# Finding the capacity threshold of eight experts: ten rounds of four or six candidates in place of eight rounds of seven

## The chip, the cores and the metric

The kernel runs on one core of a Trainium2 chip. The metric is the device time of one execution in microseconds, median of several runs. One execution was recorded by the hardware profiler; "span" is the time from its first to its last recorded instruction. The engines are TensorE (PE for its matmuls, PEld for its weight loads), VectorE (DVE), ScalarE (ACT), GpSimd (POOL) and SyncE (SP), which here only issues transfers.

## The reference, cut to what matters

64 sequences of 128 tokens with 128 features go through a layer norm, a cross-attention block with ternary weights and 8-bit activations and a residual addition. Then comes a second layer norm and a mixture of eight experts, which the change belongs to:

```python
T = tokens.shape[0]                                 # 8192
capacity = int(math.ceil(T / E * 1.25))             # 1280, E = 8
logits = tokens @ router_w.T
probs = jax.nn.softmax(logits, axis=-1)
top1_idx, top1_prob = argmax(probs), max(probs)
order = jnp.lexsort((-top1_prob, top1_idx))         # by expert, the most probable first
...
keep = (position in the expert's group) < capacity
final_e = where(keep, top1_idx, 0)                  # the rest fall back to expert 0
for e in range(E):
    h = relu(tokens @ W1[e] + b1[e]); y = h @ W2[e] + b2[e]
    out = out + where(final_e == e, y, 0)
```

A token keeps its expert if it is among the 1280 most probable tokens of that expert.

## The kernel before, in words

The program is one straight line per engine, put in order by hand. Semaphores order the engines among each other. The stages are: loading and quantising (to about 90 us), attention (to about 190 us), the quantised feed-forward block with residual, second layer norm and logits (to about 294 us), routing (to about 374 us), and the expert passes to the end.

**Routing.** After the softmax every token has a key, minus its top probability times `FULL` = 2^26, in the column of its own expert and 0 elsewhere (L1540). The sorting of the reference is replaced by a search: for each expert the kernel looks for the key value at which the count of tokens at or below it reaches the capacity. The keys are turned by TensorE (L1078) so that the 128 partitions hold eight experts times sixteen parts, 512 keys in each, once in PSUM bank 0 (read by VectorE) and once in bank 3 (read by ScalarE).

The search has `LEVELS` = 8 rounds, `level(k)` on VectorE from L1549. A round narrows the interval of each expert to one eighth: 

- There are `WAYS - 1` = 7 candidates, in the columns of `cand`. VectorE counts for four of them (`VECTOR_COUNTS`, L1546, 128x512, with the sum in `cnt`), ScalarE for three (L798, Sign of candidate minus key, with the sum in `cnt`).
- When both are done, TensorE adds the sixteen parts of each expert (L1087, `same_expert` times `cnt`) onto a row of offsets, `enough`, that an earlier matmul (L1083) has put into the same bank: minus the capacity for VectorE's counts, `T - 2 * CAP` for ScalarE's, whose sum of signs runs from -8192 to 8192. A candidate has reached the capacity where the result is at least 0.
- VectorE counts these (L1559, `reached` and `met`), makes the next candidates (L1562, from `met`, `minus_w` and `base`, which L1557 prepared while TensorE was at work), and moves the threshold `thr` (L1564).
- Both engines wait for `cand` (semaphore `s_cand`), and TensorE waits for both (`s_cnt`, `s_cnt_act`, in `count_up`).

The width of the steps is 2^26 divided by 8, by 64 and so on, to 4 in the eighth round. After it VectorE alone counts for the four single units below (L1571 to L1578), and the threshold is exact to one unit.

The constants `nth` (1, 2, 3, ...), `minus_w` and `enough` are written by GpSimd at the start of the program (L524 to L528).

**After the search** VectorE works out ties, each token's place in its expert's list and the index tables (L1596 to L1675), with a few matmuls of TensorE between. It ends with `src_of` and `slot_of`, behind which the semaphore `s_idx` lets GpSimd start.

**The expert passes.** GpSimd's queue gathers 64 tiles of 128 token rows by an indirect transfer (L587) and scatters 64 tiles of results (L594), from the 32nd gather on in turns. SyncE copies the weights of the pass's expert (L490). TensorE, ScalarE and VectorE compute 71 passes (L1131, L1138, L1147 with L816, L828, L1697, L1703, L1709).

Of the kernel before, what the change touches and what calls it, by code (L numbers as in the profile page):

```python
# [11 lines left out]
ALU = mybir.AluOpType  # L12
# [3 lines left out]
P = 128  # L16
# [9 lines left out]
T = B * S  # L26
# [6 lines left out]
CAP = int(np.ceil(T / NX * 1.25))  # L33
# [20 lines left out]
MAGIC = 12582912.0  # L54
EPS = 1e-5
FULL = 2.0 ** 26
WAYS = 8
LEVELS = 8
VECTOR_COUNTS = 4
EXP_IS_ONE = -2.0 ** -25  # L60
HT = 16
FAR = 32768
# [49 lines left out]
def xattn_moe(nc, x, ctx_in, weights, biases, router_w, W1, b1, W2, b2, out):  # L112
    rows = nc.dram_tensor("token_rows", (T, XW), F32).ap()
    with ExitStack() as stack:
        def sb(name, shape, dtype=F32):
            return stack.enter_context(nc.sbuf_tensor(name, shape, dtype))

        def sem(name):
            return stack.enter_context(nc.semaphore(name))
# [6 lines left out]
        ones = sb("ones", [P, P])  # L126
# [6 lines left out]

        nth = sb("nth", [P, WAYS - 1])
        minus_w = sb("minus_w", [P, LEVELS])
        enough = sb("enough", [1, WAYS - 1])
        tile_no_b = sb("tile_no_b", [P, TILES], BF16)
        row_no_b = sb("row_no_b", [P, P], BF16)
        part_no = sb("part_no", [P, 1])
# [77 lines left out]
        def route(n):  # L217
            return big[:, n * 512:(n + 1) * 512]
# [30 lines left out]
        by_pass = big[:, 10 * 512:10 * 512 + 4 * PASSES].rearrange("p (k a) -> p k a", a=PASSES)  # L249
        cnt = sb("cnt", [P, WAYS - 1])  # L250
        reached = sb("reached", [P, WAYS - 1])
        thr_row = sb("thr_row", [NX, NX])
        above_row = sb("above_row", [P, NX])
        met = sb("met", [P, 1])
        base = sb("base", [P, WAYS - 1])
        thr = sb("thr", [P, 1])
        cand = sb("cand", [P, WAYS - 1])
        thr8 = sb("thr8", [P, NX])
# [14 lines left out]
        s_const = sem("constants_made")  # L273
# [86 lines left out]
        s_cand = sem("candidates_ready")  # L360
# [31 lines left out]
        def bank(n, width=512, rows_=P):  # L392
            return psum[0:rows_, n, 0:width]
# [101 lines left out]
        def _(pool):  # L495
# [20 lines left out]
            for d in range(-(P // NX) + 1, P // NX):  # L516

                pool.affine_select(out=same_expert[:, :], in_=same_expert[:, :], compare_op=ALU.not_equal, fill=1.0,
                                   base=NX * d, pattern=[[-1, P]], channel_multiplier=1).then_inc(s_cc, 1)
                pool.wait_ge(s_cc, 5 + d + P // NX)  # L520
            segv = seg[:, :].rearrange("p (e t) -> p e t", e=NX)
            pool.memset(segv[:, :, 0:1], 0.0).then_inc(s_const, 1)
            for k in range(LEVELS):
                pool.memset(minus_w[:, k:k + 1], -FULL / WAYS ** (k + 1)).then_inc(s_const, 1)  # L524
            pool.memset(enough[:, 0:4], float(-CAP)).then_inc(s_const, 1)
            pool.memset(enough[:, 4:WAYS - 1], float(T - 2 * CAP)).then_inc(s_const, 1)
            pool.iota(nth[:, :], pattern=[[1, WAYS - 1]], base=1, channel_multiplier=0,
                      allow_small_or_imprecise_dtypes=True).then_inc(s_const, 1)  # L528
            for e in range(NX):
# [77 lines left out]
        def _(act):  # L607
# [17 lines left out]
            w = CJ * DC // NP  # L625
# [61 lines left out]
            w = T // XP  # L687
# [105 lines left out]
            act.wait_ge(s_vt, 2)  # L793
            for k in range(LEVELS):
                if k:
                    act.wait_ge(s_cand, k)
                for j in range(VECTOR_COUNTS, WAYS - 1):
                    m = act.activation(route(5 + j), bank(3), ACT.Sign, bias=cand[:, j:j + 1], scale=-1.0,  # L798
                                       accum_out=cnt[:, j:j + 1])
                m.then_inc(s_cnt_act, 1)  # L800
# [42 lines left out]
        def _(pe):  # L843
# [71 lines left out]
            w = T // XP  # L915
# [164 lines left out]

            def count_up(k, n):

                pe.matmul(bank(1 + k % 2, n), ones[0:1, :], enough[:, 0:n], start=True, stop=False)  # L1083
                pe.wait_ge(s_cnt, k + 1)
                if k < LEVELS:
                    pe.wait_ge(s_cnt_act, k + 1)
                pe.matmul(bank(1 + k % 2, n), same_expert[:, :], cnt[:, 0:n], start=False, stop=True  # L1087
                          ).then_inc(s_cnt2, 1)

            for k in range(LEVELS):  # L1090
                count_up(k, WAYS - 1)
            count_up(LEVELS, 4)
            pe.wait_ge(s_thr, 1)
            pe.matmul(bank(4, NX), ones[0:NX, :], thr_row[:, :], start=True, stop=True).then_inc(s_thr_s, 1)
# [69 lines left out]
        def _(dve):  # L1164
            ch = Chain(dve, s_dve)

            def do(ins):
                ch.link(ins)
                ch.join()
# [45 lines left out]
            w = CJ * DC // NP  # L1215
# [134 lines left out]
            w = T // XP  # L1350
# [180 lines left out]
            do(dve.tensor_reduce(t64[2][:, :], v3(route(1)), AX, ALU.max))  # L1531
            ch.link(dve.tensor_tensor(v3(route(1)), v3(route(1)), over_e(t64[2][:, :]), ALU.is_equal))
            ch.link(dve.memset(thr[:, :], 0.0))
            ch.link(dve.tensor_scalar(cand[:, :], nth[:, :], -FULL / WAYS, None, ALU.mult))
            dve.wait_ge(s_ex, 1)
            ch.link(dve.tensor_copy(w1b[:, :, FF:FF + NC], b1col))
            do(dve.tensor_reduce(t64[1][:, :], v3(route(4)), AX, ALU.add))
# [7 lines left out]
            def count(column, limit, form):  # L1545
                return dve.tensor_scalar(route(5 + column).bitcast(I16)[:, 0:512], key, limit, None, form, ALU.add,  # L1546
                                         accum_out=cnt[:, column:column + 1])

            def level(k):  # L1549

                w = FULL / WAYS ** (k + 1)
                for j in range(VECTOR_COUNTS):
                    m = count(j, cand[:, j:j + 1], ALU.is_le)
                m.then_inc(s_cnt, 1)
                if k + 1 < LEVELS:
                    ch.join()
                    do(dve.tensor_scalar(base[:, :], nth[:, :], -w / WAYS, thr[:, :], ALU.mult, ALU.add))  # L1557
                dve.wait_ge(s_cnt2, k + 1)
                do(dve.tensor_scalar(reached[:, :], bank(1 + k % 2, WAYS - 1), 0.0, None, ALU.is_ge, ALU.add,  # L1559
                                     accum_out=met[:, :]))  # L1560
                if k + 1 < LEVELS:
                    dve.scalar_tensor_tensor(cand[:, :], minus_w[:, k:k + 1].to_broadcast([P, WAYS - 1]), met[:, :],  # L1562
                                             base[:, :], ALU.mult, ALU.add).then_inc(s_cand, 1)
                    ch.link(dve.scalar_tensor_tensor(thr[:, :], met[:, :], -w, thr[:, :], ALU.mult, ALU.add))  # L1564
                    dve.wait_ge(s_cand, k + 1)
                else:
                    do(dve.scalar_tensor_tensor(thr[:, :], met[:, :], -w, thr[:, :], ALU.mult, ALU.add))

            for k in range(LEVELS):
                level(k)  # L1570
# [63 lines left out]
            first, start, end = spans[:, 0, :], spans[:, 1, :], spans[:, 2, :]  # L1634
# [28 lines left out]
            w = [big[:, (14 + j) * 512:(14 + j) * 512 + TILES] for j in range(2)]  # L1663
# [84 lines left out]
```

## Time and profile before

| | us |
|---|---|
| median of 3 runs | 544.47 |
| lowest and highest | 543.80, 544.93 |
| the profiled execution | 545.08 |
| its span | 543.3 |

| engine | busy us | share of the span | instructions |
|---|---|---|---|
| PE | 378.2 | 70% | 2861 |
| DVE | 377.3 | 69% | 941 |
| ACT | 353.1 | 65% | 827 |
| POOL | 197.7 | 36% | 276 |

No engine is busy all the time: these shares are averages over stages with different limits. The chain of waits, followed back from the last instruction, tells what set the end in each stage, and the timeline of a stretch shows the instructions with the idle time before each and what ended it. The profiled execution's 545.08 us stand 1.8 us above its span and 0.6 us above the median.

### The profile page before, as it was taken

The page shows a single profiled execution, that of the slowest core. Times are in us where ns is not written, and L with a number is a line of the kernel's source. Part 1 is how long each engine was busy: PE and PEld are TensorE (multiplying, and loading weights), DVE is VectorE, ACT ScalarE, POOL GpSimd, SP SyncE. Part 2 cuts the span into 40 slices and gives each one's busy share as a digit, 9 for nine tenths or more (in the row PEclk, how much of TensorE's full clock was granted, in tenths as well). Part 3 has the DMA queues.
Part 4 walks back from the last instruction along what each step waited for, and adds up shares of the span by engine and source line. Part 5 has one row for each costly group of instructions (what it writes and reads, how often), then busy time and mean ns, then how long its engine had stood idle before and what let it go on. Part 6 is the DMA issues. An engine that isn't in the chain of part 4 may idle for free.

```text
span 543.3 us, 10418 instructions
## 1 busy us (share of the span) xinstructions
PE 378.2 (70%) x2861; PEld 307.1 (57%) x2861; DVE 377.3 (69%) x941; ACT 353.1 (65%) x827; POOL 197.7 (36%) x276
## 2 busy tenths in 40 slices
PE   0370418999999889957876322233999999998940
PEld 0230005689999744426553222032999999998940
DVE  2999998478888869967898788796355555444520
ACT  1589987687878549949983443052677777776720
POOL 7300093244444300000000000003777777777774
PEclk9999999999999969978989555568799999999985
DMA  9920000000000000000336950002767666665511
GB/s 216 246 71 1 1 0 0 2 1 2 0 0 0 1 1 1 0 0 1 80 79 121 256 129 0 1 1 83 226 224 230 224 226 223 216 233 198 201 54 34
DMA packets 45137, 48.67 MB, mean 90 GB/s; under 512 B 10232, under 2 KB 32800, under 8 KB 45088
## 3 DMA queue, kind: packets, MB, share of 16 engines
q1 hardware_dynamic: 39728, 38.59, 24.0%
q0 software_dynamic: 4096, 8.46, 5.9%
q10 hardware_dynamic: 1264, 1.03, 0.7%
q8 instruction: 23, 0.38, 0.3%
q14 instruction: 26, 0.21, 0.1%
HBM read 16.20 MB, written 8.45 MB: 45 GB/s over the span
## 4 chain that ended last, share of the span: by engine, by line
PE 48%; DVE 23%; ACT 15%; DMA 5%; issue 4%; POOL 3%; SPq 0%; DVEq 0%; POOLq 0%; ACTq 0%
PE psum L1138 11%; PE psum L1147 10%; PE psum L956 6%; PE psum L972 5%; DVE big L1546 4%; PE psum L964 2%; ACT xqT L759 2%; POOL out L594 2%; DMA keys<-in_ctx 2%; ACT tok_b L759 2%; ACT big L662 2%; DMA out<-xall,src_of 2%; DVE xqT L1628 2%; DVE part L1322 2%; ACT big L619 1%
## 5 line engine op out<-in xcount | busy, mean ns | idle before, releaser
L587 POOL DMA_INDIRECT xall<-token_rows,src_of x64 | 61.7, 964 | 202.7 <-DVE slot_of L1675 183.5
L828 ACT ACTIVATE xqT<-psum,feat 128x128 f32<-128x128 f32 x284 | 81.0, 368 | 32.6 <-PE psum L1138 30.7
L1138 PE MATMUL psum<-xqT,feat 128*128 128x128 f32 x568 | 77.3, 281 | 0.0
L1147 PE MATMUL psum<-keys,xqT 128*128 x568 | 75.7, 277 | 0.3 <-issue 0.2
L1138 PEld LDWEIGHTS psum<-xqT,feat 128*128 128x128 f32 x568 | 71.4, 198 | 0.0
L594 POOL DMA_INDIRECT out<-xall,src_of x64 | 62.9, 983 | 19.5 <-issue 11.0
L1147 PEld LDWEIGHTS psum<-keys,xqT 128*128 128x128 f32 x568 | 68.9, 192 | 1.3 <-issue 0.9
L1703 DVE TENSOR_TENSOR xqT<-psum,feat 128x128 f32<-128x128 f32 x71 | 20.7, 292 | 52.2 <-PE psum L1147 51.7
L561 POOL TENSOR_TENSOR qb<-qb,arec 128x308 f32<-128x308 f32 x32 | 21.8, 699 | 64.6 <-DVE arec L1380 64.6
L972 PE MATMUL psum<-probT,keys 78*128 78x128 f32 x256 | 35.3, 285 | 1.8 <-ACT probT L724 1.8
L1697 DVE TENSOR_SCALAR xqT<-xall 128x128 f32 x71 | 25.8, 363 | 12.1 <-DMA xall<-token_rows,src_of 11.1
L972 PEld LDWEIGHTS psum<-probT,keys 78*128 78x128 f32 x256 | 32.1, 196 | 3.5 <-ACT probT L724 2.7
L1709 DVE SCALAR_TENSOR_TENSOR xall<-xqT,in_pass,xall 128x128 f32 x71 | 25.1, 353 | 11.8 <-ACT xall L822 9.1
L956 PE MATMUL psum<-keys 128*128 128x77 f32 x256 | 32.1, 277 | 1.3 <-ACT keys L609 0.9
L956 PEld LDWEIGHTS psum<-keys 128*128 128x128 f32 x256 | 30.0, 192 | 4.2 <-ACT keys L609 1.6
L724 ACT COPY probT<-psum 77x512 f32<-77x512 f32 x32 | 18.3, 576 | 21.0 <-PE psum L964 21.0
L850 PE MATMUL psum<-ident,amax 128*1 128x128 f32 x6 | 2.2, 372 | 40.6 <-DVE amax L1222 15.4
L609 ACT ACTIVATE keys<-psum,bcol,scale 128x308 f32<-128x308 f32 (+1 forms) x48 | 28.3, 658 | 3.1 <-PE psum L932 3.0
L816 ACT COPY xqT<-psum 128x128 f32<-128x128 f32 x71 | 20.5, 289 | 13.0 <-PE psum L1131 12.8
L798 ACT ACTIVATE big<-psum,cand 128x512 f32<-128x512 f32 x24 | 16.2, 683 | 18.5 <-DVE cand L1562 12.8
L1131 PE MATMUL psum<-ident,xqT 128*128 128x128 f32 x71 | 20.3, 286 | 7.9 <-DVE xqT L1697 7.9
L1546 DVE TENSOR_SCALAR_CACHE_REDUCE big<-psum,cand 128x512 int16<-128x512 f32 x36 | 24.9, 748 | 1.2 <-PE psum L1078 1.2
(301 smaller groups left out, 933.9 us busy)
## 6 DMA issues: line engine op xcount, KB each, us to landing
feat<-keys SPq DMA_DIRECT2D x71, 322.0 KB
token_rows<-xall SPq DMA_DIRECT2D x4, 1040.0 KB, 8.1
xall<-in_x SPq DMA_DIRECT2D x8, 512.0 KB, 7.3
keys<-in_L_ffn_W SPq DMA_DIRECT2D x1, 2048.0 KB, 13.2
keys<-in_L_ffn_W SPq DMA_DIRECT2D x8, 256.0 KB, 7.5
keys<-in_ctx SPq DMA_DIRECT2D x4, 462.0 KB, 6.8
xall<-token_rows,src_of POOLq DMA_INDIRECT x64
out<-xall,src_of POOLq DMA_INDIRECT x64, 2.3
```

Source lines behind the costliest of these rows:

```text
L561: pool.tensor_tensor(pr, pr, arec[:, l, :].unsqueeze(2).to_broadcast([P, GB, CT]), ALU.mult).then_inc(s_p[l], 1)
L587: pool.indirect_dma_start(xring[:, t % RING, :], None, rows, bass.IndirectOffsetOnAxis(ap=src_of[:, t:t + 1], axis=0)).then_inc(s_g[t % TU ...
L594: pool.indirect_dma_start(out_rows, bass.IndirectOffsetOnAxis(ap=src_of[:, t:t + 1], axis=0), yring[:, t % RING, :], None).then_inc(s_o[t ...
L609: return act.activation(dst, src_bank, ACT.Identity, bias=bcol[:, b:b + 1], scale=scale[:, k:k + 1])
L828: m = act.activation(hT[a % DEPTH][:, P * c:P * c + P], bank(2 + a % 2)[:, P * c:P * c + P], ACT.Relu, bias=w_now[a % AHEAD][:, FF + c:FF ...
L956: m = pe.matmul(bank(1 + l)[:, CT * b:CT * b + CT], src[n % GR][:, P * b:P * b + P], kT[l][n % GR][:, CT * b:CT * b + CT], start=True, sto ...
L972: m = pe.matmul(bank(5 + l)[:, P * b:P * b + P], ktok[l][n % (GR if l else 2)][:, P * b:P * b + P], probT[l][:, P * b:P * b + P], start=Tr ...
L1138: m = pe.matmul(bank(2 + a % 2)[:, P * c:P * c + P], w_now[a % AHEAD][:, P * c:P * c + P], gT[a % DEPTH], start=True, stop=True)
L1147: m = pe.matmul(bank(4 + a % 2, E), hT[a % DEPTH][:, P * c:P * c + P], w2s[:, bass.ds(e, 1), c, :].rearrange("p e d -> p (e d)"), start=(c ...
L1546: return dve.tensor_scalar(route(5 + column).bitcast(I16)[:, 0:512], key, limit, None, form, ALU.add, accum_out=cnt[:, column:column + 1])
L1697: dve.tensor_scalar(gn[m], xr[:, 0:E], xr[:, E:E + 1], xr[:, E + 1:E + 2], ALU.subtract, ALU.mult).then_inc(s_prep, 1)
L1709: dve.scalar_tensor_tensor(y, yt[a % 2], in_pass[:, a:a + 1], y, ALU.mult, ALU.add).then_inc(s_y, 1)
```

## The change

The rounds become ten, with a radix of their own each: two rounds that divide by seven (six candidates) and eight that divide by five (four candidates). VectorE counts for the first half of a round's candidates and ScalarE for the other half. The steps are 4 times the product of the radices still to come, so 10,937,500 in the first round, 1,562,500 in the second, then 312,500 and so on down to 20 and 4. All of them are whole units. The four single units at the end stay. The row of offsets gets three forms: for four candidates, for six, and for the four of the end, where all counts are VectorE's.

```diff
-WAYS = 8
-LEVELS = 8
-VECTOR_COUNTS = 4
+RADIX = (7, 7) + (5,) * 8
+LEVELS = len(RADIX)
+STEP = [4.0 * int(np.prod(RADIX[k + 1:])) for k in range(LEVELS)]
+WAYS = max(RADIX)
+FORMS = sorted(set(RADIX)) + [LEVELS]
...
-        enough = sb("enough", [1, WAYS - 1])
+        enough = sb("enough", [1, len(FORMS), WAYS - 1])
...
             for k in range(LEVELS):
-                pool.memset(minus_w[:, k:k + 1], -FULL / WAYS ** (k + 1)).then_inc(s_const, 1)
-            pool.memset(enough[:, 0:4], float(-CAP)).then_inc(s_const, 1)
-            pool.memset(enough[:, 4:WAYS - 1], float(T - 2 * CAP)).then_inc(s_const, 1)
+                pool.memset(minus_w[:, k:k + 1], -STEP[k]).then_inc(s_const, 1)
+            for n, radix in enumerate(FORMS[:-1]):
+                half = radix // 2
+                pool.memset(enough[:, n, 0:half], float(-CAP)).then_inc(s_const, 1)
+                pool.memset(enough[:, n, half:2 * half], float(T - 2 * CAP)).then_inc(s_const, 1)
+            pool.memset(enough[:, len(FORMS) - 1, 0:4], float(-CAP)).then_inc(s_const, 1)
...
             for k in range(LEVELS):
                 if k:
                     act.wait_ge(s_cand, k)
-                for j in range(VECTOR_COUNTS, WAYS - 1):
+                for j in range(RADIX[k] // 2, RADIX[k] - 1):
                     m = act.activation(route(5 + j), bank(3), ACT.Sign, bias=cand[:, j:j + 1], scale=-1.0,
                                        accum_out=cnt[:, j:j + 1])
...
-                pe.matmul(bank(1 + k % 2, n), ones[0:1, :], enough[:, 0:n], start=True, stop=False)
+                form = FORMS.index(RADIX[k] if k < LEVELS else LEVELS)
+                pe.matmul(bank(1 + k % 2, n), ones[0:1, :], enough[:, form, 0:n], start=True, stop=False)
...
             for k in range(LEVELS):
-                count_up(k, WAYS - 1)
+                count_up(k, RADIX[k] - 1)
...
-            ch.link(dve.tensor_scalar(cand[:, :], nth[:, :], -FULL / WAYS, None, ALU.mult))
+            ch.link(dve.tensor_scalar(cand[:, :], nth[:, :], -STEP[0], None, ALU.mult))
...
-                w = FULL / WAYS ** (k + 1)
-                for j in range(VECTOR_COUNTS):
+                w, n = STEP[k], RADIX[k] - 1
+                for j in range(n // 2):
                     m = count(j, cand[:, j:j + 1], ALU.is_le)
                 m.then_inc(s_cnt, 1)
                 if k + 1 < LEVELS:
+                    more = RADIX[k + 1] - 1
                     ch.join()
-                    do(dve.tensor_scalar(base[:, :], nth[:, :], -w / WAYS, thr[:, :], ALU.mult, ALU.add))
+                    do(dve.tensor_scalar(base[:, 0:more], nth[:, 0:more], -STEP[k + 1], thr[:, :], ALU.mult, ALU.add))
                 dve.wait_ge(s_cnt2, k + 1)
-                do(dve.tensor_scalar(reached[:, :], bank(1 + k % 2, WAYS - 1), 0.0, None, ALU.is_ge, ALU.add,
+                do(dve.tensor_scalar(reached[:, 0:n], bank(1 + k % 2, n), 0.0, None, ALU.is_ge, ALU.add,
                                      accum_out=met[:, :]))
                 if k + 1 < LEVELS:
-                    dve.scalar_tensor_tensor(cand[:, :], minus_w[:, k:k + 1].to_broadcast([P, WAYS - 1]), met[:, :],
-                                             base[:, :], ALU.mult, ALU.add).then_inc(s_cand, 1)
+                    dve.scalar_tensor_tensor(cand[:, 0:more], minus_w[:, k:k + 1].to_broadcast([P, more]), met[:, :],
+                                             base[:, 0:more], ALU.mult, ALU.add).then_inc(s_cand, 1)
```

## Rows read from the trace of the kernel before

**Rows 1.** The page: the chain that ended last, its shares by line.

```profile
PE psum L1138 11%; PE psum L1147 10%; PE psum L956 6%; PE psum L972 5%; DVE big L1546 4%; PE psum L964 2%; ACT xqT L759 2%; POOL out L594 2%; DMA keys<-in_ctx 2%; ACT tok_b L759 2%; ACT big L662 2%; DMA out<-xall,src_of 2%; DVE xqT L1628 2%; DVE part L1322 2%; ACT big L619 1%
```

**Rows 2.** GpSimd, 374 to 544 us, by line: busy us, mean ns | idle us, what ended it.

```profile
L594 POOL DMA_INDIRECT out<-xall,src_of x64 | 62.9, 983 | 19.5 <-issue 11.0 <-DMA out<-xall,src_of 4.9 <-DVE xall L1709 3.7
```

**Rows 3.** Timeline, last stage: start us, duration us, instruction [idle before it <- releaser].

```profile
374.38 1.14 POOL L587 DMA_INDIRECT xall<-token_rows,src_of  x1 [183.47 <-DVE slot_of L1675]
...
536.72 0.97 POOL L594 DMA_INDIRECT out<-xall,src_of  x1 [0.30 <-DMA out<-xall,src_of]
```

**Rows 4.** Chain of waits through one round: start us, duration us, what.

```profile
310.73 2.75 DVE big L1546 x8
313.48 0.04 issue
313.52 0.61 PE psum L1087 x2
...
314.24 0.18 DVE reached L1559 x2
```

**Rows 5.** Timeline of the first round.

```profile
302.31 0.75 DVE L1546 TENSOR_SCALAR_CACHE_REDUCE big<-psum,cand 128x512 int16<-128x512 f32 x1 [1.21 <-PE psum L1078]
...
303.16 0.69 ACT L798 ACTIVATE big<-psum,cand 128x512 f32<-128x512 f32 x1 [5.64 <-PE psum L1078]
...
305.00 0.08 DVE L1546 DVE_READ_ACCUMULATOR big<-psum,cand 128x1 f32 x1
...
305.07 0.21 ACT L798 ACTIVATION_READ_ACCUMULATOR big<-psum,cand 128x1 f32 x1
...
305.42 0.57 PE L1087 MATMUL psum<-cnt,same_expert 128*128 128x7 f32 x2 [1.78 <-ACT big L798]
...
306.68 0.74 DVE L1546 TENSOR_SCALAR_CACHE_REDUCE big<-psum,cand 128x512 int16<-128x512 f32 x1
```

**Rows 6.** Timeline of the second and third rounds.

```profile
308.49 0.21 ACT L798 ACTIVATION_READ_ACCUMULATOR big<-psum,cand 128x1 f32 x1
308.69 0.09 DVE L1546 DVE_READ_ACCUMULATOR big<-psum,cand 128x1 f32 x1
...
309.50 0.60 PE L1087 MATMUL psum<-cnt,same_expert 128*128 128x7 f32 x2 [2.99 <-DVE big L1546]
...
310.69 0.75 DVE L1546 TENSOR_SCALAR_CACHE_REDUCE big<-psum,cand 128x512 int16<-128x512 f32 x1
...
311.94 0.20 ACT L798 ACTIVATION_READ_ACCUMULATOR big<-psum,cand 128x1 f32 x1
...
312.04 0.09 DVE L1546 DVE_READ_ACCUMULATOR big<-psum,cand 128x1 f32 x1
...
314.71 0.75 DVE L1546 TENSOR_SCALAR_CACHE_REDUCE big<-psum,cand 128x512 int16<-128x512 f32 x1
```

**Rows 7.** Timeline: the eighth round's first count, and the first of the single units.

```profile
330.79 0.75 DVE L1546 TENSOR_SCALAR_CACHE_REDUCE big<-psum,cand 128x512 int16<-128x512 f32 x1
...
334.92 0.75 DVE L1546 TENSOR_SCALAR_CACHE_REDUCE big<-psum,cand 128x512 int16<-128x512 f32 x1
```

**Rows 8.** The groups of 302 to 339 us: VectorE's small instructions of a round.

```profile
L1562 DVE SCALAR_TENSOR_TENSOR cand<-minus_w,met,base 128x7 f32<-128x7 f32 x7 | 1.6, 226 | 0.2
L1559 DVE TENSOR_SCALAR_CACHE_REDUCE reached<-psum 128x7 f32<-128x7 f32 x8 | 1.3, 166 | 5.4 <-PE psum L1087 5.4
```

**Rows 9.** Chain of waits ahead of the routing: ScalarE to TensorE.

```profile
293.38 0.59 ACT big L788
293.98 0.04 issue
```

**Rows 10.** Timeline of GpSimd after its constants.

```profile
66.65 1.76 POOL L550 TENSOR_TENSOR qb<-feat 128x704 f32<-128x704 f32 x1 [46.99 <-ACT feat L609]
```

**Rows 11.** Busy us by engine (instructions), then TensorE's granted clock, DMA share, GB/s.

```profile
301.00:303.00 2.00, 1.84 (x8) 1.56 (x8) 0.79 (x4) 0.00 (x0) 0.00 (x0) 0.50 1.05 379
...
318.70:322.80 4.10, 1.12 (x4) 1.00 (x4) 3.43 (x15) 2.16 (x7) 0.00 (x0) 0.50 0.01 3
```

**Rows 12.** Timeline: the same fp32 matmul of 128 columns at two granted clocks.

```profile
381.18 0.47 PE L1131 MATMUL psum<-ident,xqT 128*128 128x128 f32 x1 [1.17 <-DVE xqT L1697]
...
387.61 0.27 PE L1131 MATMUL psum<-ident,xqT 128*128 128x128 f32 x1
```

## The prediction, made before the changed kernel was run

> **What bounds the kernel now.** I read the page first. The engines' shares say little, since no engine passes 70%. The chain of waits says more: the counting of the search, L1546, is 4% of the chain that ended last [rows 1], so the search lies on the path that sets the end. Then I asked whether time won there reaches the end, so I read the last stage backwards. GpSimd's queue starts its first gather at 374.38, released by `slot_of`, and its last scatter ends at 536.72 + 0.97 = 537.69 [rows 3]. That is 163.31 us for 64 gathers and 64 scatters, 1.28 us each. The 64 scatters have 19.5 us of idle time before them, 0.30 each, which is what a mere issue costs, whatever the releaser's name [rows 2]. So this queue is full from its start to its end. Nothing else sets the length of the stage, and the whole stage moves with `slot_of`.
>
> Between the search and `slot_of` the chain is VectorE's, instruction behind instruction, with a few short matmuls. The transfers of expert weights that run beside the search are over by its fifth round: 3 GB/s from 318.7 on [rows 11]. So what the search gains, `slot_of` gains, and with it the end.
>
> **A round as it is.** The third round's first count starts at 310.69, the fourth's at 314.71: 4.02 us [rows 6]. Rows 4 show who sets it: four counts of VectorE and TensorE's sum. ScalarE's three counts end earlier and its name is not in the chain. I cut the round at TensorE's start, 313.52:
> - Counting: 313.52 - 310.69 = 2.83 us [rows 4, 6]. The pitch of VectorE's counts is 0.67, and TensorE starts 0.14 after the start of the last accumulator read.
> - The fixed part: from 313.52 to the next count at 314.71, 1.19 us. That is the two passes of the matmul (0.72 to `reached` at 314.24), then `reached`, `cand` and the hand-over (0.47) [rows 4, 6].
>
> The eighth round is 4.13 long, 330.79 to 334.92, since its candidates for the single units are made one after another [rows 7]. The first takes 306.68 - 302.31 = 4.37 [rows 5].
>
> **What the change makes of it, round by round.**
>
> First round, three and three. ScalarE starts late, at 303.16, because it waits for the second set of transposes, and its three counts end at 305.07 + 0.21 = 305.28. TensorE starts at 305.42, with ScalarE as the releaser; VectorE's fourth count was over at 305.08 [rows 5]. One count less on VectorE wins nothing. Gain 0.
>
> Second round, three and three. VectorE's third read starts at 308.69, which puts TensorE at 308.83. ScalarE's third read ends at 308.49 + 0.21 = 308.70, and with the 0.14 from its end to TensorE seen in the first round that is 308.84 [rows 5, 6]. Before it was 309.50. Gain 0.66.
>
> Rounds of two and two. Counted from 310.69, VectorE's second read starts at 312.04 (+1.35), so TensorE could start at +1.49. ScalarE's second read ends at 311.94 + 0.20 (+1.45), so TensorE could start at +1.59 with the same 0.14 [rows 5, 6]. The later one counts, 1.59 in place of 2.83: gain 1.24, and such a round is 1.59 + 1.19 = 2.78 us.
>
> The third to the eighth round of before become such rounds: 6 x 1.24 = 7.44. Two more rounds are added at 2.78: 5.56. The long hand-over to the single units now stands behind the tenth round and costs what it did. In sum 0 + 0.66 + 7.44 - 5.56 = 2.54 us less: 32.61 us of search (302.31 to 334.92) become 30.07.
>
> The uncertain term is the 0.14 from ScalarE's last accumulator read to TensorE, seen once. Another hand-over of this pair, L788 to a matmul, took 0.04 [rows 9]. At 0.04 VectorE would set the rounds of two and two at +1.49, 0.10 less each. With eight of them the gain would be 3.34. The other end is the 0.35 between the start of that read and TensorE [rows 5], in case the signal follows the read's end less closely than it did there: 0.21 more in eight rounds, 1.68, which leaves 0.86. I take 0.14, since it is this very instruction's.
>
> The instructions with six and four columns in place of seven I cost as before: `cand` takes 0.226 and `reached` 0.166 at seven columns [rows 8], and at most three columns of some 1 ns go. `base` stays hidden: in a short round it starts with the second read at +1.35 and TensorE's answer comes at +2.3. The row of offsets is put in place right behind the sum before, over a microsecond ahead of need. GpSimd's five more writes of constants lie ahead of an idle time of 46.99 us [rows 10]. The counts cost the same whatever the values of the candidates.
>
> A rule speaks against more and shorter rounds. The three small VectorE instructions of a round take 0.17 to 0.23 us each for at most seven columns [rows 8], so nearly all of it is a fixed price, and two rounds more pay it twice. The Trainium skill says why (VectorE: DVE Perf Modes, "The TRN2 errata"): each instruction pays a fixed latency between instructions, and many small tiles pay it per tile. The trace agrees in kind, but not in size: from the Trainium skill's table, 58 or 120 cycles and the columns, I estimate 0.07 us for `cand` and 0.13 for `reached`, so 0.20 where the rows have 0.47 with the hand-over. By the Trainium skill's figures the two added rounds would cost 0.54 less and the gain would be 3.1 us.
>
> **The time.** The profiled execution of 545.08 becomes 542.54. It lies 0.61 above the median of 544.47; with the same 2.54 the median becomes 541.93, 0.47% less. The measurement of this kernel can tell about 0.2%, 1.1 us, from no change.
>
> **The rivals.**
> - *ScalarE's hand-over is short.* VectorE sets the rounds, the gain is 3.34 and the time 541.1. For it: the 0.04 of rows 9. Against it: no accumulator is read there. Chance 0.16.
> - *The fixed part grows, and the change is slower.* In a round of two and two both engines end within 0.1 us, TensorE waits for both, and both wait for the same `cand`. The 1.33 us in which nobody counts (1.19 and 0.14) come ten times in place of eight. If ScalarE is released or read out later than in the rows, so that a short round takes over 2.78 + 2.54 / 8 = 3.10 us, the gain is gone. At 3.3 us per round the time would be 544.47 - 2.54 + 8 x 0.52 = 546.1. Against it: the third to seventh rounds of before agree to 0.01 us, and the slowest hand-over seen gives 2.99. Chance 0.05.
> - *The gain is given back behind the search.* If some transfer, and not `slot_of`, decided when GpSimd's queue moves, or its scatters came to wait for results, up to 2.5 us would be lost and the time would be 544.5. For it: 16 of the 64 scatters name an earlier scatter's landing as their releaser [rows 2]. Against it: each such wait is 0.30, as an issue with no wait. Chance 0.09.
> - *TensorE's clock comes back in the search.* It is at 0.50, 1.2 GHz, in the search, though TensorE was busy for 1.84 of 2 us just before it [rows 11]. A busy share of 1.12 in 4 becomes 1.12 in 2.8. At 2.4 GHz the fp32 matmul of 128 columns takes 0.27 in place of 0.47 [rows 12], so up to 0.2 a round, 2 us in all, and a time of 539.9. The Trainium skill (TensorE: Matmul & The Clock Gate, Part 1) has the clock throttled by default and released by activity; the rows of 301 to 303 show more activity than the new rounds will have, without a release. Chance 0.02.
>
> The forecast, a gain of 2.0 to 3.0, has 0.68.
>
> **How the numbers follow.** Faster by over 0.2% needs a time under 543.4: the forecast, the first and the last rival and a small part of the others, 0.87. Within 0.2%: 0.09. Slower: 0.04. The range of 8 in 10 reaches from the short hand-over with the median's own scatter of 0.5 below it, 540.6, to the long hand-over, 544.47 - 0.86 = 543.6.
>
> **What would show it.** In the profile after: ten rounds; the first 4.37 from first count to first count, the second 3.35, the others 2.78, the tenth 2.89; TensorE's L1087 released by ScalarE's L798 in all of them, where VectorE's L1546 released it eight times in nine before; 30.1 us from the first count to the first of the single units; the first gather 2.5 us earlier after the start of the search than now; the stage of GpSimd's queue unchanged at 163 us. The prediction is wrong in its main term if a short round takes over 3.1 us, and wrong in its path if the search is 2.5 us shorter and the time is not.

## The result and the profile after

The changed kernel takes 541.99 us in the median of 9 runs (541.48 to 542.93), the kernel before beside it 544.77 (9 runs, 543.45 to 546.08). The ratio is 0.9954, with an interval of 0.9942 to 0.9966: 1.9 to 3.2 us less. Forecast were 541.9 us. In a second comparison, on another occasion, the ratio was 0.9947 (0.9929 to 0.9964).

Here is the new search in the chain of waits of the changed kernel, one short round (start us, duration us, what). It answers to [rows 4].

```profile
311.97 1.46 ACT big L803 x4
313.42 0.14 issue
313.56 0.57 PE psum L1093 x2
314.13 0.03 issue
...
314.25 0.18 DVE reached L1566 x2
314.43 0.02 issue
314.45 0.23 DVE cand L1569
...
314.71 1.46 ACT big L803 x4
```

The counting in the chain is now ScalarE's (L803, L798 before), 1.46 us, where it was VectorE's, 2.75. After it comes an `issue` gap, time in which the engine waited for nothing that the profile shows, of 0.14 and no longer one of 0.04. From 311.97 to 314.71 a round takes 2.74 us. The waits of the changed kernel in the stretch from 298 to 340 us say the same of all ten rounds; the eleventh entry is the four single units (waiting engine <- engine waited for: us, times, longest).

```profile
PE psum L1093 <- ACT big L803: 17.5, 10, 2.3
...
PE psum L1093 <- DVE big L1552: 3.0, 1, 3.0
```

The timeline of the first round and the start of the second, third and fourth of the changed kernel answers to [rows 5, 6]:

```profile
301.54 0.75 DVE L1552 TENSOR_SCALAR_CACHE_REDUCE big<-psum,cand 128x512 int16<-128x512 f32 x1 [1.21 <-PE psum L1083]
...
302.39 0.69 ACT L803 ACTIVATE big<-psum,cand 128x512 f32<-128x512 f32 x1 [5.64 <-PE psum L1083]
...
304.30 0.21 ACT L803 ACTIVATION_READ_ACCUMULATOR big<-psum,cand 128x1 f32 x1
304.62 0.50 PEld L1093 LDWEIGHTS psum<-cnt,same_expert 128*128 128x128 f32 x2 [1.84 <-DVE big L1552]
304.65 0.57 PE L1093 MATMUL psum<-cnt,same_expert 128*128 128x6 f32 x2 [1.78 <-ACT big L803]
...
305.81 0.75 DVE L1552 TENSOR_SCALAR_CACHE_REDUCE big<-psum,cand 128x512 int16<-128x512 f32 x1
...
309.23 0.75 DVE L1552 TENSOR_SCALAR_CACHE_REDUCE big<-psum,cand 128x512 int16<-128x512 f32 x1
```

The first round is 4.27 us, the second 3.42, then come seven of 2.74 and the last of 2.85. Note that two engines are named at 304.62 and 304.65: the weight load gives VectorE as its releaser, the matmul ScalarE. ScalarE is the one that decides: VectorE's last read had ended at 303.64, ScalarE's ends at 304.51, and the weight load starts 0.11 behind that.

The stage behind is what it was. The first line answers to [rows 2] and the others, from the timeline of GpSimd, to [rows 3]:

```profile
L599 POOL DMA_INDIRECT out<-xall,src_of x64 | 63.0, 985 | 19.5 <-issue 11.3 <-DMA out<-xall,src_of 4.6 <-DVE xall L1716 3.7
```

```profile
370.72 1.13 POOL L592 DMA_INDIRECT xall<-token_rows,src_of  x1 [179.23 <-DVE slot_of L1682]
...
533.04 0.97 POOL L599 DMA_INDIRECT out<-xall,src_of  x1 [0.31 <-DMA out<-xall,src_of]
```

The granted clock stayed at 0.50, 1.2 GHz, through the short rounds (columns as in [rows 11]):

```profile
320.20:325.70 5.50, 2.14 (x8) 1.99 (x8) 4.02 (x20) 2.92 (x9) 0.00 (x0) 0.50 0.00 0
```

The spans of the two profiled executions differ by 543.3 - 539.6 = 3.7 us, more than the medians. Cut at the same places:

| stretch, us | before | after | gain |
|---|---|---|---|
| to the first count | 302.31 | 301.54 | 0.77 |
| search, to the first count of the single units | 32.61 | 29.72 | 2.89 |
| from there to GpSimd's first gather | 39.46 | 39.46 | 0.00 |
| GpSimd's queue, first to last | 163.31 | 163.29 | 0.02 |
| behind it | 5.61 | 5.59 | 0.02 |

The 0.77 lies ahead of everything that was changed, and in another execution of the same changed kernel this part ends at 302.57. It is no gain. The change's own gain in the trace is 2.89 us.

### The profile page after: what moved, and what is told of

Same layout as the page of the kernel before. It is cut to its first block, busy times and chain, and to the rows that moved or that the text cites. A ratio compares the mean times of both kernels' runs of the same rounds, so it can differ in the third digit from the quotient of the medians.

```text
span 539.6 us, 10429 instructions
## 1 busy us (share of the span) xinstructions
PE 377.7 (70%) x2869; PEld 306.5 (57%) x2869; DVE 372.4 (69%) x931; ACT 352.6 (65%) x823; POOL 197.4 (37%) x281
## 4 chain that ended last, share of the span: by engine, by line
PE 48%; DVE 22%; ACT 17%; DMA 5%; issue 4%; POOL 3%; SPq 1%; DVEq 0%; POOLq 0%; ACTq 0%
PE psum L1144 11%; PE psum L1153 11%; PE psum L961 6%; PE psum L977 5%; ACT big L803 3%; PE psum L969 2%; POOL out L599 2%; ACT tok_b L764 2%; DMA keys<-in_ctx 2%; ACT xqT L764 2%; ACT big L667 2%; DMA out<-xall,src_of 2%; DVE xqT L1635 2%; DVE part L1328 2%; ACT big L624 2%
## 5 line engine op out<-in xcount | busy, mean ns | idle before, releaser
L977 PEld LDWEIGHTS psum<-probT,keys 78*128 78x128 f32 x256 | 31.7, 193 | 3.5 <-ACT probT L729 2.7
L803 ACT ACTIVATE big<-psum,cand 128x512 f32<-128x512 f32 x22 | 14.9, 683 | 17.3 <-DVE cand L1569 11.7
L1028 PE MATMUL psum<-tok_b,f1T 128*128 128x512 bf16 x64 | 24.3, 380 | 2.2 <-ACT keys L757 1.3
```

Of the source, the lines that this page charges most:

```text
L977: m = pe.matmul(bank(5 + l)[:, P * b:P * b + P], ktok[l][n % (GR if l else 2)][:, P * b:P * b + P], probT[l][:, P * b:P * b + P], start=Tr ...
L1028: pe.matmul(bank(b), f1T[:, 0, P * c:P * c + P], tok_b[:, g4(i)], start=True, stop=False)
```

## The experiments

All are edits of the changed kernel. The table holds what the timelines and the comparisons gave; "search" runs from the first count to the first of the single units, the rounds in it are measured from first count to first count on VectorE. The ratio is to the kernel before, run on the same chip as the row's kernel, with its interval. The rows come from several chips, on which the kernel before had medians of 544.38 to 544.95.

| kernel | rounds, us | search | first gather to last scatter | median | ratio |
|---|---|---|---|---|---|
| before | 4.37, 4.01, 5 x 4.02, 4.13 | 32.61 | 163.31 | 544.77 | |
| changed | 4.27, 3.42, 7 x 2.74, 2.85 | 29.72 | 163.29 | 541.99 | 0.9954 (0.9942 to 0.9966) |
| changed, again | 4.27, 3.41, 7 x 2.74, 2.86 | 29.72 | 163.17 | 542.26 | 0.9947 (0.9929 to 0.9964) |
| share undone | 4.11, 4.01, 7 x 3.33, 3.45 | 34.90 | 163.25 | 547.27 | 1.0043 (1.0029 to 1.0058) |
| nine of seven | 4.27, 7 x 3.42, 3.53 | 31.74 | 163.34 | 543.07 | 0.9962 (0.9947 to 0.9978) |
| sixteen of three | 2.93, 2.39, 13 x 2.07, 2.19 | 34.37 | 163.19 | 546.43 | 1.0035 (1.0017 to 1.0053) |
| four empty rounds | 4.27, 3.42, 11 x 2.74, 2.85 | 40.68 | 163.24 | 552.27 | 1.0145 (1.0114 to 1.0175) |
| two and one | 4.27, 3.42, 9 x 2.66, 2.77 | 34.40 | 163.88 | 547.49 (one run) | |
| one semaphore | 4.20, 3.35, 7 x 2.68, 2.79 | 29.09 | 163.09 | 541.66 | 0.9934 (0.9916 to 0.9952) |
| from an eighth | 4.37, 2.65, 7 x 2.74, 2.86 | 29.06 | 163.45 | 540.98 | 0.9925 (0.9909 to 0.9940) |
| both | 4.30, 2.66, 7 x 2.68, 2.79 | 28.49 | 162.96 | 540.77 | 0.9932 (0.9914 to 0.9949) |
| no join | 4.18, 3.32, 7 x 2.65, 2.86 | 28.93 | 163.29 | 540.44 | 0.9934 (0.9921 to 0.9948) |
| all three | 4.11, 8 x 2.59, 2.79 | 27.61 | 163.48 | 538.48 | 0.9895 (0.9880 to 0.9910) |

From the first count of the single units to the first gather it is 39.43 to 39.46 us in every one of them.

**The share undone.** Is the gain the radices', or the equal share's?

```diff
-                half = radix // 2
+                half = radix // 2 + 1
...
-                pool.memset(enough[:, n, half:2 * half], float(T - 2 * CAP)).then_inc(s_const, 1)
+                pool.memset(enough[:, n, half:radix - 1], float(T - 2 * CAP)).then_inc(s_const, 1)
...
-                for j in range(RADIX[k] // 2, RADIX[k] - 1):          # ScalarE
+                for j in range(RADIX[k] // 2 + 1, RADIX[k] - 1):
...
-                for j in range(n // 2):                               # VectorE
+                for j in range(n // 2 + 1):
```

> The changed kernel with its ten rounds, but VectorE counts for four of six and three of four candidates, ScalarE for two and one. My theory: a round costs the later engine's counts plus a fixed part, so both the radices and the equal share are needed. From the rows: first round 3.99 us (VectorE's four counts, 2.83, plus 1.16), second 3.99, seven of 3.31, the last 3.42; search 34.6 us from the first count to the first of the single units, 4.9 longer than the changed kernel's 29.7 and 2.0 longer than before's 32.6; time 546.8. Rival, the radices alone make the gain (ScalarE's share is covered either way): search near 29.7, time 542.

The search became 34.90 us, 0.3 more than expected, and the kernel slower than before. Of the 0.3, 0.12 are in the first round (4.11 for 3.99); the rest is 0.02 to 0.03 in each of the others. VectorE's three counts make a round of 3.33. So these rounds of five pay only if no engine has to count more than two. The matmul that ends a round names VectorE again:

```profile
312.39 0.59 PE L1093 MATMUL psum<-cnt,same_expert 128*128 128x4 f32 x2 [2.23 <-DVE big L1552]
```

**Nine rounds of seven.** Few rounds, equal share.

```diff
-RADIX = (7, 7) + (5,) * 8
+RADIX = (7,) * 9
```

> Nine rounds of six candidates, three on each engine, in place of ten of six or four. My theory (later engine's counts plus fixed part): first round 4.27, seven of 3.42, the last 3.52; search 31.7 us, 2.0 longer than the changed kernel's, 0.9 shorter than before's; time 543.9. Rival, what counts is the number of rounds, since the fixed part of a round grows when the engines end together: one round less than ten would make it shorter than 29.7 and the time under 542.

31.74 against 31.7: the round of three and three is 3.42 wherever it stands, and one round less doesn't make up for it. Nine rounds of three and three in place of eight of four and three are worth 0.87 us; the rest of the 2.89 comes from going down to five. In that 0.87 the equal share and the smaller radix are not told apart: eight candidates, four and four, were not run. By the times this kernel can't be told from the changed one, since the intervals overlap; by the traces it can.

**Sixteen rounds of three.** The shortest round there is, in which the fixed part weighs most. (`WAYS` keeps room for the four single units.)

```diff
-RADIX = (7, 7) + (5,) * 8
+RADIX = (3,) * 16
...
-WAYS = max(RADIX)
+WAYS = max(RADIX + (5,))
```

> Sixteen rounds of two candidates, one on each engine. It puts weight on the fixed part. My theory (a round is 1.40 + 0.67 for each candidate of ScalarE): first round 2.92, fourteen of 2.07, the last 2.18; search 34.1 us, 4.4 longer than the changed kernel's; time 546.3. Rival, the fixed part grows when rounds are short (TensorE's two matmuls with their weight loads, 1.09 us in a round of 2.07, or base no longer hidden): rounds of 2.3 us or more, search over 37, time over 549.

A round is 2.07 us, as the straight line through 2.74 and 3.42 has it. The fixed part doesn't grow when rounds get short. The search was 0.3 longer than expected by a single stall in the second round. In its timeline the accumulator read of `reached` starts 0.42 us after the instruction it belongs to, where it is 0.08 or 0.09 in the others, with no releaser:

```profile
306.42 0.16 DVE L1566 TENSOR_SCALAR_CACHE_REDUCE reached<-psum 128x2 f32<-128x2 f32 x1 [0.71 <-PE psum L1093]
306.84 0.08 DVE L1566 DVE_READ_ACCUMULATOR reached<-psum 128x1 f32 x1 [0.25 <-issue]
```

What stalled it I don't know.

**Four empty rounds.** What is a microsecond of the search worth at the end?

```diff
-RADIX = (7, 7) + (5,) * 8
+RADIX = (7, 7) + (5,) * 12
```

> Fourteen rounds: two of six candidates and twelve of four, with steps four rounds wider than needed, so that the first rounds find nothing and the result stays the same. It measures what a microsecond of the search is worth at the end. My theory: every microsecond reaches the end, since GpSimd's queue is full from its first gather on. Search 29.7 + 4 x 2.74 = 40.7 us, time 542.0 + 11.0 = 553.0 us (8.2 over before), GpSimd's queue 163.3 us as ever. Rival, part of it is given back or absorbed behind the search (a transfer or TensorE's clock sets the last stage): less than 10 of the 11 us in the time. The rounds that find nothing should cost what the others do.

The search grew by 10.96 us. In the profiled execution the span is 549.9, 10.3 more than the changed kernel's. The missing 0.6 lie ahead of the search, whose first count comes at 300.97 in place of 301.54. From there to the end nothing is absorbed: GpSimd starts at 381.08, again 39.43 behind the first single unit, and its queue is as long as ever.

```profile
381.08 1.13 POOL L592 DMA_INDIRECT xall<-token_rows,src_of  x1 [189.86 <-DVE slot_of L1682]
...
543.35 0.97 POOL L599 DMA_INDIRECT out<-xall,src_of  x1 [0.30 <-DMA out<-xall,src_of]
```

The medians differ by 10.3 us, and the ratio allows 6.2 to 9.5 us over the kernel before, where the traces' searches give 8.07 (40.68 - 32.61). So by the times alone a loss of a microsecond or so could not be excluded; the row of 39.43 and the queue exclude it.

**Two and one.** The same counts on VectorE, one less on ScalarE.

```diff
-RADIX = (7, 7) + (5,) * 8
+RADIX = (7, 7) + (4,) * 10
...
-                pool.memset(enough[:, n, half:2 * half], float(T - 2 * CAP)).then_inc(s_const, 1)
+                pool.memset(enough[:, n, half:radix - 1], float(T - 2 * CAP)).then_inc(s_const, 1)
...
-                for j in range(n // 2):
+                for j in range(RADIX[k] // 2):
```

> Twelve rounds: two of six candidates as in the changed kernel, then ten of three candidates, two on VectorE and one on ScalarE, so that VectorE ends last. It tells apart what the hand-over from ScalarE costs against that from VectorE at the same number of counts. My theory: VectorE's second read lets TensorE start at +1.49 where ScalarE's did at +1.59, so a round is 2.64 us where two and two take 2.74; search 34.2 us. Rival, the end of a round is set by TensorE's two waits or by both engines being released together, and not by which one ends last: 2.74 or more a round.

A round took 2.66, with VectorE as the releaser of TensorE; 0.08 less than with ScalarE's second count. The timeline of one round:

```profile
315.32 0.75 DVE L1552 TENSOR_SCALAR_CACHE_REDUCE big<-psum,cand 128x512 int16<-128x512 f32 x1
...
316.67 0.08 DVE L1552 DVE_READ_ACCUMULATOR big<-psum,cand 128x1 f32 x1
...
316.80 0.50 PEld L1093 LDWEIGHTS psum<-cnt,same_expert 128*128 128x128 f32 x2 [1.64 <-DVE big L1552]
316.80 0.59 PE L1093 MATMUL psum<-cnt,same_expert 128*128 128x3 f32 x2 [1.56 <-DVE big L1552]
...
317.51 0.16 DVE L1566 TENSOR_SCALAR_CACHE_REDUCE reached<-psum 128x3 f32<-128x3 f32 x1 [0.63 <-PE psum L1093]
```

TensorE starts 1.48 after the round's start (1.49 was expected), weight load and matmul at once, and `reached` follows 0.71 later. The search took 34.40 us, 0.2 more than expected, because a round is 2.66 and not 2.64. The time of this kernel is that of one execution, and nothing rests on it.

**One semaphore.** Where do the 0.14 behind ScalarE's read come from?

```diff
-                m.then_inc(s_cnt_act, 1)                              # ScalarE
+                m.then_inc(s_cnt, 1)
...
-                pe.wait_ge(s_cnt, k + 1)
-                if k < LEVELS:
-                    pe.wait_ge(s_cnt_act, k + 1)
+                pe.wait_ge(s_cnt, 2 * k + (2 if k < LEVELS else 1))
```

> The changed kernel, but VectorE and ScalarE both add to one semaphore and TensorE waits once for the sum, in place of one semaphore and one wait for each. It asks where the 0.14 us from ScalarE's last accumulator read to TensorE come from. My theory: they belong to ScalarE's read, whose signal comes after the end that is recorded: rounds stay at 2.74, search at 29.7, time 542.0. Rival, they are the second wait in front of the matmul: about 0.09 less in each of ten rounds, rounds of 2.65, search 28.8, time 541.1.

My theory fell here, at least for the larger part. The chain of waits of this kernel shows 0.04 where the changed kernel has 0.14:

```profile
310.10 1.46 ACT big L803 x4
311.56 0.04 issue
311.60 0.60 PE psum L1091 x2
```

A round is 2.68, 0.06 less and not 0.09. The other 0.03 or so are a matter of where one cuts: with two waits the weight load starts 0.11 after ScalarE's read and the matmul 0.03 behind it (304.62 and 304.65 above), with one wait both start 0.05 after it (311.60). In both cases `reached` starts 0.71 to 0.73 after the weight load. So the second wait costs 0.06 in these rounds, where ScalarE, which it waits for, ends last. It doesn't matter how long the first wait has been fulfilled: 0.02 us in the short rounds, 0.87 in the first, which went from 4.27 to 4.20.

**From an eighth, and both.** The largest of eight probabilities is at least 1/8, so the keys (without their sign) begin at 2^23; `LEAST` is a little below, and 8 x 5^9 steps of four cover what is left up to 2^26. The first round now has four counts on VectorE and three on ScalarE; its row of offsets is split accordingly, as in the edit of two and one.

```diff
-RADIX = (7, 7) + (5,) * 8
+RADIX = (8,) + (5,) * 9
+LEAST = 2.0 ** 23 - 4096
...
-            ch.link(dve.memset(thr[:, :], 0.0))
-            ch.link(dve.tensor_scalar(cand[:, :], nth[:, :], -STEP[0], None, ALU.mult))
+            ch.link(dve.memset(thr[:, :], -LEAST))
+            ch.link(dve.tensor_scalar(cand[:, :], nth[:, :], -STEP[0], -LEAST, ALU.mult, ALU.add))
```

> A version meant to be faster than both. The top probability of eight is at least an eighth, so the search need not start at 0 but at 2^23 - 4096, and 8 x 5^9 steps of four units are enough: first a round of seven candidates, four on VectorE and three on ScalarE (free, since in the first round ScalarE starts late and ends last anyway), then nine of four. The second round of six candidates becomes one of four. My theory: 4.27 + 8 x 2.74 + 2.85 = 29.0 us of search, 0.68 less than the changed kernel, time 541.3. Rival: the fourth count on VectorE in the first round is not free, 4.4 or more for it, and the gain is under 0.5.

29.06 us, 0.66 less. The first round is 4.37 as before the change, but the second is 2.65, together 7.02 where 4.27 and 2.74 make 7.01: the fourth count in the first round is free. The first round is 0.10 longer than expected, and ScalarE starts the second one 0.10 ahead of VectorE, so that VectorE ends that round.

> The version from an eighth (a round of seven, nine of four candidates) together with the one semaphore. The one semaphore took 0.06 to 0.07 off each of ten rounds. My theory: the two add up, since one changes a round's candidates and the other its hand-over: first round 4.3, nine others of 2.68 with the last 2.79, search 28.4 us (29.06 and 29.09 with either alone), 1.3 less than the changed kernel and 4.2 less than before; time 540.5, ratio 0.992. Rival: in the first round VectorE's four counts now end close to ScalarE's three and set it, so that the one semaphore wins nothing there: 28.5.

28.49 us of search: that is the rival's number (28.5; the theory had 28.4), but not in the round that the rival named. The two edits add up but for one round, and it is the second and not the first: there the one semaphore wins nothing (2.66 and 2.65), VectorE being last. Here are VectorE's last read and TensorE's start in that round, with two waits (from an eighth) and with one (both):

```profile
307.51 0.08 DVE L1553 DVE_READ_ACCUMULATOR big<-psum,cand 128x1 f32 x1
...
307.64 0.50 PEld L1094 LDWEIGHTS psum<-cnt,same_expert 128*128 128x128 f32 x2 [1.74 <-DVE big L1553]
```

```profile
307.02 0.08 DVE L1551 DVE_READ_ACCUMULATOR big<-psum,cand 128x1 f32 x1
...
307.16 0.50 PEld L1092 LDWEIGHTS psum<-cnt,same_expert 128*128 128x128 f32 x2 [1.74 <-DVE big L1551]
```

From one to the other it is 0.13 and 0.14. So two waits cost nothing more than one when the engine that the first of them waits for ends last, and two and one, whose TensorE starts 0.13 after that read with both waits, says the same. Whether it is enough to swap TensorE's two waits was not run.

The median is 540.77 and the ratio 0.9932 (0.9914 to 0.9949). That these two are faster than the changed kernel (0.7 and 1.2 us by their searches) rests on the traces: the intervals of their ratios (0.9909 to 0.9940 and 0.9914 to 0.9949) overlap the changed kernel's second one, 0.9929 to 0.9964.

The changed kernel, run again beside them:

> The changed kernel itself, unaltered, beside the two above on the same chip and with the same runs of the kernel before: 542.0 us and a ratio near 0.995, a search of 29.7 us in ten rounds of 4.27, 3.42, eight times 2.74 with the last 2.85. If the ratio lies above 0.998, part of the gain measured first was the chip's and not the kernel's.

0.9947, and a search of 29.72 to the hundredth.

**No join, and all three.** If a second wait has a price on TensorE, it may have one on VectorE. There `base` is waited for, and behind that wait stands the one for TensorE's sum.

```diff
-                    do(dve.tensor_scalar(base[:, 0:more], nth[:, 0:more], ...))
+                    ch.link(dve.tensor_scalar(base[:, 0:more], nth[:, 0:more], ...))
```

`do` makes VectorE wait for the instruction's end at once. With `link` the wait behind `reached` covers both.

> The changed kernel, but VectorE no longer waits for the end of its own base instruction before it waits for TensorE's sum; the next wait for its own instructions, behind reached, covers base as well. In the changed kernel reached starts 0.71 us after TensorE's weight load in nine rounds and 0.63 in the tenth and for the single units, where there is no base and no such wait. My theory: it is the same price as with TensorE's two waits, a second wait in front of an instruction: 0.08 less in nine of ten rounds, rounds of 2.66, search 29.0, time 541.3. Rival, it is base itself, which VectorE runs in the meantime, and the rounds stay at 2.74.

2.65, so 0.09 less in each of the nine rounds that have a `base`. The timeline of one of them, with `base` still there, over long before TensorE's sum comes (`reached` starts 0.63 after the weight load):

```profile
312.88 0.22 DVE L1564 TENSOR_SCALAR base<-nth,thr 128x4 f32<-128x4 f32 x1
313.09 0.50 PEld L1093 LDWEIGHTS psum<-cnt,same_expert 128*128 128x128 f32 x2 [1.63 <-DVE big L1552]
...
313.72 0.16 DVE L1566 TENSOR_SCALAR_CACHE_REDUCE reached<-psum 128x4 f32<-128x4 f32 x1 [0.62 <-PE psum L1093]
```

> All three together: from an eighth with 8 x 5^9 steps, one semaphore for both counts, and no wait for base. My theory: they add up, rounds of 2.60, search 28.49 - 9 x 0.08 = 27.8 us, 1.9 less than the changed kernel and 4.8 less than before; time 540.0, ratio 0.991. Rival, without the second wait on one side the other engine's own start-up shows, and less than half of the 0.08 is won: search 28.1 or more.

A search of 27.61 us with rounds of 2.59, 0.15 less than the changed kernel's; the two prices add up, and the rival fell. The search is 0.2 shorter than expected, since the first round went down to 4.11: 0.09 for the wait and 0.10 because its `thr` is not late here (more on that below). The chain of waits of this kernel:

```profile
312.32 1.46 ACT big L804 x4
313.78 0.04 issue
313.82 0.60 PE psum L1092 x2
314.42 0.02 issue
314.44 0.18 DVE reached L1565 x2
314.62 0.03 issue
314.65 0.23 DVE cand L1568
```

It is the fastest that I ran: 538.48 us, a ratio of 0.9895 (0.9880 to 0.9910), 4.9 to 6.5 us less than before, and its interval doesn't touch that of the changed kernel. The search gives 5.00 of it. The time expected was 540.0. In the profiled execution another 1.9 us lie ahead of the search, whose first count comes at 300.45 in place of 302.31; none of the three edits adds or takes away an instruction there.

## Why the prediction was right

*The search is on the path, and what it gains reaches the end.* Right, and shown with nearly four times the gain in the other direction, by the four empty rounds (10.96 us against 2.89).

*First round: gain 0.* 0.10, from 4.37 to 4.27. The matmul started when it was expected to, 3.11 us after the first count, released by ScalarE. The 0.10 are VectorE's: in the kernel before the update of `thr` starts 0.28 after `cand` in this one round and 0.14 in all others, and in the changed kernel 0.14 here too. From the timeline of the kernel before, whose `cand` starts at 306.32:

```profile
306.58 0.69 ACT L798 ACTIVATE big<-psum,cand 128x512 f32<-128x512 f32 x1 [1.31 <-DVE cand L1562]
306.60 0.16 DVE L1564 SCALAR_TENSOR_TENSOR thr<-met,thr 128x1 f32<-128x1 f32 x1
```

It is late in four of the five kernels whose VectorE counts four in the first round (before, share undone, from an eighth, both, but not all three), and in none of the others. Why is open.

*Second round: gain 0.66.* 3.42 in place of 4.01, 0.59. The two together give 0.69 for 0.66: in the kernel before ScalarE began the second round 0.10 ahead of VectorE, because of that late `thr`, and in the changed kernel they begin together.

*Short rounds: 2.78.* 2.74. The counting part was right to the hundredth, 313.56 - 311.97 = 1.59, ScalarE last. The fixed part of 1.19 was 1.15. It was not the columns: with three columns and VectorE last it is 1.18. The 1.19 had been cut at the matmul of a round that VectorE ends, and the 0.14 at the matmul of one that ScalarE ends, whose weight load starts 0.03 before it. Added together they count these 0.03 twice.

*The uncertain term, 0.14 for ScalarE's hand-over.* The size was right and its reason wrong. I had put it down to this very instruction, the accumulator read. With one wait it is 0.04 to 0.05, the number of [rows 9], which I had weighed and set aside. Of the 0.09 that go, 0.06 are the price of TensorE's second wait, and the round gains them; 0.03 are the matmul's start behind its weight load. For the sum it made no difference, as the changed kernel has both waits. It would have made one for whoever wanted to shorten the round.

*In sum* 2.89 in the trace for 2.54: 0.03 from the first two rounds and 0.04 in each of the eight short ones, which together took 22.03 for 22.35.

*The time itself* is met more closely than the working deserves: 541.99 for 541.93. The kernel before came out 0.30 higher beside it (544.77 for 544.47), and the gain in the medians was 0.24 larger (2.78 for 2.54). That the two cancel is luck.

*Fixed prices.* `cand` takes 0.226 us with seven columns [rows 8] and 0.223 in the mean of the changed kernel, with four or six, and the fixed part of a round is the same from two candidates to seven. The Trainium skill's rule (VectorE: DVE Perf Modes, "The TRN2 errata") is that an instruction which reads SBUF pays a fixed extra latency whatever its size. By `cand` the trace agrees with it in that. The gain of 3.1 us that its figures gave lies nearer to 2.89 than my 2.54, but not for its reason: the small instructions didn't get cheaper.

*The rivals.* The short hand-over didn't come by itself, but it came when one wait was taken away. A growing fixed part was excluded at 2, 4 and 6 candidates. Nothing was given back: the stretch between search and first gather agrees to 0.03 us in all kernels. TensorE's clock stayed at 0.50 in the short rounds.

## What to carry to other kernels

In a search whose rounds need an answer from another engine, a round costs a fixed part and a price per candidate on the busiest engine, here 1.40 us and 0.67. Write that line down from one round of the trace and minimise it over the radix: per bit gained, the rounds measured here cost 2.07 / 1.58 = 1.31 us with radix 3, 2.74 / 2.32 = 1.18 with 5, 3.42 / 2.81 = 1.22 with 7 and 4.02 / 3 = 1.34 with the old 8 and its unequal share. The line is the one for ScalarE last and two waits; with VectorE last a round of two counts was 0.08 shorter. Before one believes in such a gain, the stage behind has to be read: here it counted in full because that stage starts with the search's result and kept its length, 163.0 to 163.9 us in every kernel.

## What the runs showed of the hardware that was not expected

- Two waits in a row ahead of an instruction, of which the second is the late one, cost more than one: 0.06 us on TensorE (rounds of 2.74 and 2.68) and 0.09 on VectorE (2.74 and 2.65), though the first wait was fulfilled by then, by 0.02 us or 0.87 on TensorE and by some 0.7 on VectorE. Together they were 0.15 (2.59). Where the first was the late one, TensorE's second wait cost nothing (rounds of 2.65 and 2.66 with two waits and with one).
- VectorE and ScalarE counted 128x512 values from PSUM, with a sum, at the same pitch of 0.67 us. ScalarE's read of the sum lasts 0.20 and VectorE's 0.08, but in a row of counts neither adds to the pitch.
- TensorE's part of a round, from the weight load to the next engine's start, was 0.71 to 0.73 us with two, three, four, six and seven columns alike, at 1.2 GHz; 0.63 where VectorE had only one wait.
